# Sixteen-head attention with a ternary-weight layer: input tiles loaded from another queue, in four buffers instead of three

## The chip, the cores and the metric

One Trainium2 chip, eight cores. Each core runs the same program on one of the eight batch elements, and nothing is exchanged between cores. The metric is the device time of the slowest core, in microseconds (us), as the median over runs. Engines are called PE (TensorE, matmul), PEld (its weight loads), DVE (VectorE), ACT (ScalarE), POOL (GpSimd) and SP (SyncE). SP does no arithmetic here: it issues transfers. Each engine takes its instructions strictly in the order of its own program, and an instruction that waits holds up all behind it.

## The reference

Per batch element, with S = E = 2048, 16 heads of 128:

```python
xn = layernorm(x)                                    # over E, no scale or shift
q, k, v = xn @ wq, xn @ wk, xn @ wv                  # 16 heads of 128
q, k = rope(q), rope(k)
attn = softmax(q @ k.T / sqrt(128) + causal) @ v @ wo
s = mean(abs(weight)); w_t = clip(round(weight / s), -1, 1)
ffn = xn @ (w_t * s).T + bias
out = x + attn + ffn
```

## The kernel before

Five lists of closures are built, one for each engine, and then played back, so the order of the Python calls is the order of each engine's program. There are two phases. Phase 1 makes the transposed layernorm `xnT`, does projections and attention for the 16 heads, and in the shadow of the heads makes the ternary weights. Phase 2 (L961 and L977) multiplies out both output products and isn't touched.

**Layernorm.** `plan_ln_tile(tt)` (L218) handles 128 rows of x: a 1 MB load into `xst[tt % 3]`, four statistics instructions and an aggregate on DVE (L233 to L242), Ln and Exp on ACT (L251, L258), the subtract and multiply to bf16 `xnn[tt % 2]` on DVE (L267), and a DMA transpose from `xnn` into `xnT`, issued by SP. The load is issued by POOL. It waits only for its buffer (`xst_free`: the L267 of the tile that last used it) and for the buffer's own semaphore.

**Heads 0 and 1** are interleaved with the layernorm (L726 to L760). p0(c) and p1(c) are the projections of chunk c (512 columns) for heads 0 and 1: K, Q and V in that order, 16 matmuls each, alternating between the banks `pA` and `pB`. p0(c) has to wait for the four transposes of its chunk. After p1(c) comes b0(c), the layernorm of the four tiles of chunk c+1, and then the attention of chunk c. SP also issues a DMA transpose of V (`vh<-prawv`, here called tv) for each head and chunk, as soon as DVE has evacuated V (L515).

**Heads 2 to 15** (L777) have the order: p(0), p(1), attention(0), background(0), background(1), p(2), attention(1), background(2), p(3), attention(2), attention(3), background(3). The background of heads 2 to 5 is `plan_quantA_tile` (L292): load 1 MB of the layer's weight, take its absolute sum on ACT (L306), one tile for each chunk. The background of heads 6 to 13 is `plan_quantB_tile` (L368), two tiles a head: load 1 MB again, three DVE instructions (L391, L395, L401), then on SP a DMA transpose (`wtTs<-wtbf`) and, once that has landed, a store. Sixteen tiles go through each of the two.

**Who waits behind these.** In DVE's program the three instructions of a quantB tile stand between the masks of attention(c-1) (L617) and the evacuation of K of the next chunk (L515). The V projection of that chunk writes the same bank as its K projection, so PE waits until K is evacuated. In ACT's program a quantA tile stands between two attentions' exponentials (L606). In SP's program tv of chunk c stands ahead of all that background(c) issues.

**Head weights.** `plan_head_weights` (L420) has POOL load the wq, wk and wv slices of a head, with a cast from f32 to bf16, in the same POOL program as the tile loads. Each waits for the load before it on its semaphore.

Of the kernel before, what the change touches and what calls it, by code (L numbers as in the profile page):

```python
# [8 lines left out]
F32 = mybir.dt.float32  # L9
# [30 lines left out]
def build_nc():  # L40
# [26 lines left out]
    with ctx:  # L67
# [21 lines left out]
        biasbc = sb("biasbc", [128, E], BF16)  # L89
        ctx1 = ExitStack()  # L90
        sb1 = lambda n_, s_, d_: ctx1.enter_context(nc.sbuf_tensor(n_, s_, d_))
        xst = [sb1(f"xst{i}", [128, E], F32) for i in range(3)]
        xnn = [sb1(f"xnn{i}", [128, E], BF16) for i in range(2)]
        wtbf = [sb1("wtbf0", [128, E], BF16)] * 4
        wtTs = [sb1("wtTs0", [128, NT * 128], BF16)] * 4
# [40 lines left out]
        def dma(engname, sem_name, make_out_in, extra_waits=(), ordered=True):  # L136
            prev = cnt[sem_name] if ordered else 0
            ws = tuple(extra_waits)

            @on(engname)  # L140
            def _(e, sem_name=sem_name, prev=prev, ws=ws, make_out_in=make_out_in):
                for s_, v_ in ws:
                    if v_:
                        e.wait_ge(sems[s_], v_)  # L144
                if prev:
                    e.wait_ge(sems[sem_name], prev)  # L146
                out, in_, tp = make_out_in()
                if tp:
                    e.dma_start_transpose(out, in_).then_inc(sems[sem_name], 16)
                else:  # L150
                    e.dma_start(out=out, in_=in_).then_inc(sems[sem_name], 16)  # L151
            return bump(sem_name, 16)

        for dst, src in [(c2, c2_d), (s2, s2_d), (tri, tri_d), (onc, onc_d),
                         (oncf, oncf_d), (onrf, onrf_d), (onm, onm_d)]:
            dma("sync", "c", (lambda dst=dst, src=src: (dst[:, :], src, False)),
                ordered=False)
        consts_c = cnt["c"]
        dma("gpsimd", "bias", (lambda: (biasb[:, :], bias_d, False)),
            ordered=False)  # L160
        dma("gpsimd", "bias", (lambda: (onr[:, :], onr_d, False)),
            ordered=False)
        bias_v = cnt["bias"]

        @on("vector")
        def _(e):
# [43 lines left out]
        def _(e):  # L210
            e.wait_ge(sems["c"], consts_c)

        xst_free = [("dv", 0), ("dv", 0), ("dv", 0)]
        xnn_free = [("txn", 0), ("txb", 0)]
        ln_state = {"prev_aggr": 0}
        ln_prev = [0, 0, 0]

        def plan_ln_tile(tt):  # L218
            b = tt % 3
            b2 = tt % 2  # L220
            xs = "x%d" % b
            my_x = dma("gpsimd", xs,
                       (lambda tt=tt, b=b: (xst[b][:, :],
                        bass.AP(x_d.tensor, tt * 128 * E, [[E, 128], [1, E]]), False)),
                       extra_waits=[xst_free[b]])

            @on("vector")
            def _(e, b=b, xs=xs, my_x=my_x, prev_aggr=ln_state["prev_aggr"]):
                e.wait_ge(sems[xs], my_x)
                if prev_aggr:  # L230
                    e.wait_ge(sems["dv"], prev_aggr)
                for j in range(3):
                    e.bn_stats(st6[:, 6 * j:6 * j + 6], xst[b][:, 512 * j:512 * (j + 1)])  # L233
                e.bn_stats(st6[:, 18:24], xst[b][:, 1536:2048]).then_inc(sems["dv"], 1)
            dv_stats = bump("dv")

            @on("vector")
            def _(e, b=b, dv_stats=dv_stats, prev=ln_prev[b]):
                e.wait_ge(sems["dv"], dv_stats)
                if prev:  # L240
                    e.wait_ge(sems["dv"], prev)
                e.bn_aggr(mv[b][:, :], st6[:, :]).then_inc(sems["dv"], 1)  # L242
            dv_aggr = bump("dv")
            ln_state["prev_aggr"] = dv_aggr

            @on("scalar")
            def _(e, b=b, dv_aggr=dv_aggr, prev=ln_prev[b]):
                e.wait_ge(sems["dv"], dv_aggr)
                if prev:
                    e.wait_ge(sems["dv"], prev)  # L250
                e.activation(out=rstd[b][:, :], in_=mv[b][:, 1:2], func=AF.Ln,  # L251
                             bias=epsv[:, :]).then_inc(sems["ac"], 1)
            ac_ln = bump("ac")

            @on("scalar")
            def _(e, b=b, ac_ln=ac_ln):
                e.wait_ge(sems["ac"], ac_ln)
                e.activation(out=rstd[b][:, :], in_=rstd[b][:, :], func=AF.Exp,  # L258
                             scale=-0.5).then_inc(sems["ac"], 1)
            ac_rstd = bump("ac")  # L260

            @on("vector")
            def _(e, b=b, b2=b2, ac_rstd=ac_rstd, xf=xnn_free[b2]):
                e.wait_ge(sems["ac"], ac_rstd)
                if xf:
                    e.wait_ge(sems[xf[0]], xf[1])
                e.tensor_scalar(out=xnn[b2][:, :], in0=xst[b][:, :], scalar1=mv[b][:, 0:1],  # L267
                                scalar2=rstd[b][:, :], op0=ALU.subtract,
                                op1=ALU.mult).then_inc(sems["dv"], 1)
            dv_xn = bump("dv")  # L270
            xst_free[b] = ("dv", dv_xn)
            ln_prev[b] = dv_xn

            txs = "txn" if tt % 2 == 0 else "txb"
            xnn_free[b2] = (txs, dma("sync", txs,
                              (lambda tt=tt, b2=b2: (
                                  bass.AP(xnT, tt * 128, [[NT * S, 128], [S, NT], [1, 128]]),
                                  xnn[b2][:, :], True)),
                              extra_waits=[("dv", dv_xn)]))

        plan_ln_tile(0)
        plan_bias_copies()
        for tt in range(1, 4):
            plan_ln_tile(tt)
        xnT_ready = 16 * (NT // 2)

        qa_ac = [0] * NT
# [2 lines left out]
        quantB_state = {"prev_sub": 0}  # L290

        def plan_quantA_tile(qt):  # L292
            b = qt % 3
            b2 = qt % 2
            xs = "x%d" % b
            my_x = dma("gpsimd", xs,
                       (lambda qt=qt, b=b: (xst[b][:, :],
                        bass.AP(wf_d.tensor, qt * 128 * E, [[E, 128], [1, E]]), False)),
                       extra_waits=[xst_free[b]])

            @on("scalar")
            def _(e, qt=qt, b=b, b2=b2, xs=xs, my_x=my_x):
                e.wait_ge(sems[xs], my_x)
                e.wait_ge(sems["txn"], xnT_ready)
                e.wait_ge(sems["txb"], xnT_ready)
                e.activation(out=xnn[b2][:, :], in_=xst[b][:, :], func=AF.Abs,  # L306
                             accum_out=accw[:, qt:qt + 1]).then_inc(sems["ac"], 1)
            qa_ac[qt] = bump("ac")
            xst_free[b] = ("ac", qa_ac[qt])
# [56 lines left out]
            return bump("dv")  # L366

        def plan_quantB_tile(qt, thr_dv):  # L368
            b = qt % 3
            xs = "x%d" % b  # L370
            my_x = dma("gpsimd", xs,
                       (lambda qt=qt, b=b: (xst[b][:, :],
                        bass.AP(wf_d.tensor, qt * 128 * E, [[E, 128], [1, E]]), False)),
                       extra_waits=[xst_free[b]])

            wtbf_free = (("tw%d" % ((qt - 1) % 2)), qb_tw[qt - 1]) if qt >= 1 else None
            prev_sub = quantB_state["prev_sub"]
# [42 lines left out]
        def plan_head_weights(h, gate_pe):  # L420
            out = {}
            hb = h % 2
            for wd, dsts, s_ in ((wq_d, wslq, "wq"), (wk_d, wslk, "wk"), (wv_d, wslv, "wv")):
                if DBG_NO_WSL:
                    out[s_] = cnt[s_]
                    continue
                out[s_] = dma("gpsimd", s_,
                              (lambda wd=wd, dst=dsts[hb], h=h: (dst[:, :],
                               bass.AP(wd.tensor, h * 128, [[E, 128], [E * 128, NT], [1, 128]]),
                               False)),  # L430
                              extra_waits=[("pe", gate_pe)])
            return out
# [38 lines left out]
        def make_head(h):  # L471
# [224 lines left out]

            def plan_background(c, h=h):
                if h == 0 and c < CH - 1:
                    for t2 in range(4 * (c + 1), 4 * (c + 1) + 4):
                        plan_ln_tile(t2)  # L700
                if do_quant and n_heads >= 14:
                    if 2 <= h <= 5:
                        plan_quantA_tile(4 * (h - 2) + c)
                    elif h == 6 and c == 0:
                        quant_thr_dv[0] = plan_quant_reduce()
                        rs_gate_pe_extra[0] = nonlocal_holder.get("rs_pe", 0)
                        plan_quantB_tile(0, quant_thr_dv[0])
                    elif 6 <= h <= 13 and c % 2 == 0 and not (h == 6 and c == 0):
                        plan_quantB_tile(2 * (h - 6) + c // 2, 0)
# [390 lines left out]
```

## Time and profile before

| | us |
|---|---|
| median of 2 runs | 1821.25 (1814.53 to 1827.96) |
| the profiled execution, device time | 1812.49 |
| its slowest core (core 0), first to last instruction | 1810.9 |
| its fastest core (core 2) | 1793.1 |
| PE busy in that core 0 | 1527.9 (84%) |
| DVE busy | 760.1 (42%) |
| ACT busy | 478.3 (26%) |

Times in the rows are microseconds from the start of the core's span. A row of the timeline has the start, the time taken, the engine, the line, the operation, what is written `<-` what is read, and how many instructions are merged; brackets give the idle time before it and what ended it. SPq and the like are the instructions that issue transfers, and their time is that of issuing, not of the transfer. All plain transfers are issued from L151 and all DMA transposes from L149.

### The profile page before, as it was taken

The page shows a single profiled execution, that of the slowest core. Times are in us where ns is not written, and L with a number is a line of the kernel's source. Part 1 is how long each engine was busy: PE and PEld are TensorE (multiplying, and loading weights), DVE is VectorE, ACT ScalarE, POOL GpSimd, SP SyncE. Part 2 cuts the span into 40 slices and gives each one's busy share as a digit, 9 for nine tenths or more (in the row PEclk, how much of TensorE's full clock was granted, in tenths as well). Part 3 has the DMA queues.
Part 4 walks back from the last instruction along what each step waited for, and adds up shares of the span by engine and source line. Part 5 has one row for each costly group of instructions (what it writes and reads, how often), then busy time and mean ns, then how long its engine had stood idle before and what let it go on. Part 6 is the DMA issues. An engine that isn't in the chain of part 4 may idle for free. (4 is left out here: it accounts for less than half of the span.)

```text
span 1810.9 us, 29591 instructions; the slowest of 8 cores (1793.1 to 1810.9 us)
## 1 busy us (share of the span) xinstructions
PE 1527.9 (84%) x9096; PEld 880.1 (49%) x9096; DVE 760.1 (42%) x1559; ACT 478.3 (26%) x837; POOL 101.2 (6%) x118
## 2 busy tenths in 40 slices
PE   0515459999999899989999999999919999999999
PEld 0202224444444344434444444444408888888888
DVE  3516253544535447456465474454302222222222
ACT  1001125345454351443433524514500000000000
POOL 2000001101100100010010000000000000000000
PEclk9857679999999999999999999999969999999999
DMA  9994536547366783673644734600084687786772
GB/s 203 165 104 63 86 73 111 78 101 114 72 116 70 122 134 78 89 108 95 101 88 92 121 79 56 88 21 7 10 179 110 147 190 161 171 170 133 156 158 86
DMA packets 350420, 194.93 MB, mean 108 GB/s; under 512 B 240193, under 2 KB 338498, under 8 KB 343874
## 3 DMA queue, kind: packets, MB, share of 16 engines
q0 software_dynamic: 139072, 92.29, 32.6%
q1 hardware_dynamic: 157730, 63.53, 19.5%
q10 hardware_dynamic: 53472, 37.23, 7.1%
q8 instruction: 84, 1.38, 0.3%
q14 instruction: 62, 0.51, 0.1%
HBM read 177.28 MB, written 32.51 MB: 116 GB/s over the span
## 5 line engine op out<-in xcount | busy, mean ns | idle before, releaser
L606 ACT ACTIVATE et<-pC,bias 128x512 bf16<-128x512 f32 (+3 forms) x240 | 149.9, 625 | 591.3 <-PE pC L593 590.4
L643 PE MATMUL pF<-et,onms 128*128 128x512 bf16 (+3 forms) x640 | 226.3, 355 | 38.1 <-DVE et L617 23.3
L593 PE MATMUL pC<-qTh,kTh 128*128 128x512 bf16 (+3 forms) x240 | 84.3, 351 | 112.0 <-ACT et L606 112.0
L500 PE MATMUL pA<-xnT,wslk 128*128 128x512 bf16 x480 | 119.3, 405 | 66.0 <-DMA xnT<-xnn 65.7
L617 DVE TENSOR_TENSOR et<-et,trim 128x128 bf16<-128x128 bf16 x256 | 56.7, 225 | 273.6 <-ACT et L606 270.4
L961 PE MATMUL pA<-wtc,xnT 128*128 128x256 bf16 x1024 | 123.9, 275 | 13.3 <-DMA wtc<-wtT_scr 13.1
L645 PE MATMUL pG<-et,vh 128*128 128x512 bf16 x376 | 133.9, 360 | 0.0
L977 PE MATMUL pA<-woc,oTh 128*128 128x256 bf16 x896 | 109.7, 275 | 27.3 <-DMA oTh<-outT_scr 27.3
L606 ACT ACTIVATE et<-pD,bias 128x512 bf16<-128x512 f32 (+3 forms) x208 | 130.7, 628 | 3.8 <-PE pD L593 3.3
L643 PEld LDWEIGHTS pF<-et,onms 128*128 128x128 bf16 x640 | 63.2, 99 | 137.6 <-issue 91.7
L961 PE MATMUL pB<-wtc,xnT 128*128 128x256 bf16 x1024 | 122.6, 273 | 0.0
L1000 DVE TENSOR_TENSOR osl<-pA,xsl 128x256 f32<-128x256 f32 x64 | 27.2, 424 | 224.3 <-PE pA L977 129.0
L606 ACT ACTIVATE et<-pH,bias 128x512 bf16<-128x512 f32 (+1 forms) x192 | 118.5, 617 | 4.6 <-PE pH L593 3.9
L961 PEld LDWEIGHTS pA<-wtc,xnT 128*128 128x128 bf16 x1024 | 100.7, 99 | 26.1 <-issue 13.7
L500 PE MATMUL pB<-xnT,wslk 128*128 128x512 bf16 x480 | 108.8, 379 | 0.2
L500 PE MATMUL pA<-xnT,wslv 128*128 128x512 bf16 x480 | 108.8, 379 | 0.0
L500 PE MATMUL pA<-xnT,wslq 128*128 128x512 bf16 x480 | 108.8, 379 | 0.0
L500 PE MATMUL pB<-xnT,wslq 128*128 128x512 bf16 x480 | 108.8, 379 | 0.0
L500 PE MATMUL pB<-xnT,wslv 128*128 128x512 bf16 x480 | 108.8, 379 | 0.0
L500 PEld LDWEIGHTS pA<-xnT,wslk 128*128 128x128 bf16 x480 | 47.7, 103 | 125.6 <-issue 81.0
L977 PE MATMUL pB<-woc,oTh 128*128 128x256 bf16 x896 | 108.3, 272 | 0.0
L977 PEld LDWEIGHTS pA<-woc,oTh 128*128 128x128 bf16 x896 | 88.3, 99 | 38.4 <-issue 27.8
(99 smaller groups left out, 1869.2 us busy)
## 6 DMA issues: line engine op xcount, KB each, us to landing
xst<-wf POOLq DMA_DIRECT2D x32, 1024.0 KB, 10.8
xst<-x POOLq DMA_DIRECT2D x16, 1024.0 KB, 18.0
xsl<-x SPq DMA_DIRECT2D x128, 128.0 KB, 4.1
wtc<-wtT_scr ACTq DMA_DIRECT2D x16, 1024.0 KB, 11.4
woc<-wo POOLq DMA_DIRECT2D x16, 1024.0 KB, 13.4
y<-osl ACTq DMA_DIRECT2D x128, 128.0 KB, 3.6
wslq<-wq POOLq DMA_DIRECT2D x16, 512.0 KB, 10.8
wslk<-wk POOLq DMA_DIRECT2D x16, 512.0 KB, 13.8
```

Source lines behind the costliest of these rows:

```text
L500: e.matmul(pp[:, 0:CW], wsl[:, it * 128:(it + 1) * 128], bass.AP(xnT, it * S + c * CW, [[NT * S, 128], [1, CW]]), start=(it == 0), stop=False)
L593: e.matmul(pc_[:, col0:CW], kTh[hb][:, kt * 128:(kt + 1) * 128], bass.AP(qTh[hb], cs0 + col0, [[S, 128], [1, n]]), start=True, stop=True). ...
L606: e.activation(out=et[slot][:, col0:CW], in_=pc_[:, col0:CW], func=AF.Exp, scale=INV_SQRT_D, bias=bias3[:, :]).then_inc(sems["ac"], 1)
L617: e.tensor_tensor(out=et[slot][:, col0:col0 + 128], in0=et[slot][:, col0:col0 + 128], in1=tri[:, :], op=ALU.mult).then_inc(sems["dv"], 1)
L643: e.matmul(pF[:, col0:CW], onm[:, :], et[slot][:, col0:CW], start=(kt == 0), stop=(kt == nkt - 1))
L645: e.matmul(pv[:, col0:CW], vh[hb][:, kt * 128:(kt + 1) * 128], et[slot][:, col0:CW], start=(kt == 0), stop=(kt == nkt - 1)).then_inc(sems[ ...
L961: e.matmul(pp[:, 0:W2], bass.AP(xnT, it * S + tt * 128, [[NT * S, 128], [1, 128]]), wtc[ecb][:, it * W2:(it + 1) * W2], start=(it == 0), s ...
L977: mm = e.matmul(pp[:, 0:W2], lh, woc[ecb][:, it * W2:(it + 1) * W2], start=False, stop=(it == NT - 1))
L1000: e.tensor_tensor(out=osl[ob][:, :], in0=pp[:, 0:W2], in1=xsl[tb][:, :], op=ALU.add).then_inc(sems["dv"], 1)
```

## The change

- `xst` has four buffers in place of three (tile number modulo 4). `mv` and `rstd` stay at three.
- All loads into `xst`, of x and of the layer's weight, go through a new `plan_x_load` and are issued by SP in place of POOL. They have the same kind of waits as before: the buffer's last reader, and the buffer's semaphore.
- The loads of x tiles 0 to 3 stand first in SP's program, ahead of the constants (two of 1 MB each and five small ones). In b0(c) the four loads stand together, ahead of the four tiles' transposes.
- In quantA and quantB the load stands in SP's program where the tile is planned: behind tv of the chunks projected so far, ahead of the tile's own transpose and store.
- POOL now issues only the bias, the head weights and, in phase 2, wo. The head weights go in the order k, q, v in place of q, k, v.

```diff
-        xst = [sb1(f"xst{i}", [128, E], F32) for i in range(3)]
+        xst = [sb1(f"xst{i}", [128, E], F32) for i in range(4)]
...
+        xst_free = [("dv", 0), ("dv", 0), ("dv", 0), ("dv", 0)]
+
+        def plan_x_load(tt, src_d=x_d):
+            b = tt % 4
+            return dma("sync", "x%d" % b,
+                       (lambda tt=tt, b=b, src_d=src_d: (xst[b][:, :],
+                        bass.AP(src_d.tensor, tt * 128 * E, [[E, 128], [1, E]]), False)),
+                       extra_waits=[xst_free[b]])
+
+        xl03 = [plan_x_load(tt) for tt in range(4)]
         for dst, src in [(c2, c2_d), (s2, s2_d), (tri, tri_d), (onc, onc_d),
...
-        def plan_ln_tile(tt):
-            b = tt % 3
+        def plan_ln_tile(tt, my_x=None):
+            b = tt % 4
+            b3 = tt % 3
             b2 = tt % 2
             xs = "x%d" % b
-            my_x = dma("gpsimd", xs,
-                       (lambda tt=tt, b=b: (xst[b][:, :],
-                        bass.AP(x_d.tensor, tt * 128 * E, [[E, 128], [1, E]]), False)),
-                       extra_waits=[xst_free[b]])
+            if my_x is None:
+                my_x = plan_x_load(tt)
...
         def plan_quantA_tile(qt):
-            b = qt % 3
+            b = qt % 4
...
-            my_x = dma("gpsimd", xs,
...
+            my_x = plan_x_load(qt, src_d=wf_d)
...
         def plan_quantB_tile(qt, thr_dv):
-            b = qt % 3
+            b = qt % 4
             xs = "x%d" % b
-            my_x = dma("gpsimd", xs,
...
+            my_x = plan_x_load(qt, src_d=wf_d)
...
-            for wd, dsts, s_ in ((wq_d, wslq, "wq"), (wk_d, wslk, "wk"), (wv_d, wslv, "wv")):
+            for wd, dsts, s_ in ((wk_d, wslk, "wk"), (wq_d, wslq, "wq"), (wv_d, wslv, "wv")):
...
                 if h == 0 and c < CH - 1:
-                    for t2 in range(4 * (c + 1), 4 * (c + 1) + 4):
-                        plan_ln_tile(t2)
+                    t2s = list(range(4 * (c + 1), 4 * (c + 1) + 4))
+                    mxs = [plan_x_load(t2) for t2 in t2s]
+                    for t2, mx in zip(t2s, mxs):
+                        plan_ln_tile(t2, mx)
```

## Rows read from the trace of the kernel before

**Rows 1.** The page, busy tenths of PE and its granted clock in 40 slices.

```profile
PE   0515459999999899989999999999919999999999
PEclk9857679999999999999999999999969999999999
```

**Rows 2.** Windows: length, busy of PE, PEld, DVE, ACT, POOL, clock, DMA share, GB/s.

```profile
78.00:132.00 54.00, 2.56 (x9) 1.15 (x9) 16.70 (x29) 4.89 (x14) 2.12 (x4) 0.52 1.04 119
159.00:208.00 49.00, 7.09 (x25) 2.75 (x24) 17.25 (x30) 7.65 (x18) 2.11 (x4) 0.56 0.93 131
```

**Rows 3.** Timeline of the start, up to the first projection.

```profile
1.07 0.39 SPq L151 DMA_DIRECT2D c<-c2t  x1
14.23 1.88 DVE L233 BATCH_NORM_STATS2 st<-xst 128x6 f32<-128x512 f32 x3 [13.00 <-DMA xst<-x]
20.65 26.18 SPq L149 DMA_TRANSPOSE xnT<-xnn  x4
53.55 6.32 PE L500 MATMUL pA<-xnT,wslk 128*128 128x512 bf16 x15 [31.23 <-DMA xnT<-xnn]
```

**Rows 4.** Timeline of b0(0), the layernorm of tiles 4 to 7.

```profile
50.65 1.63 POOL L151 DMA_DIRECT2D xst<-x  x3
78.13 1.87 DVE L233 BATCH_NORM_STATS2 st<-xst 128x6 f32<-128x512 f32 x3
83.90 0.53 POOL L151 DMA_DIRECT2D xst<-x  x1 [31.62 <-DVE xnn L267]
107.70 1.35 DVE L267 TENSOR_SCALAR xnn<-xst,mv,rstd 128x2048 bf16<-128x2048 f32 x1 [11.46 <-DMA xnT<-xnn]
132.24 6.22 PE L500 MATMUL pA<-xnT,wslk 128*128 128x512 bf16 x15 [20.51 <-DMA xnT<-xnn]
```

**Rows 5.** Timeline of b0(2), the layernorm of tiles 12 to 15.

```profile
237.81 1.87 DVE L233 BATCH_NORM_STATS2 st<-xst 128x6 f32<-128x512 f32 x3
257.42 1.35 DVE L267 TENSOR_SCALAR xnn<-xst,mv,rstd 128x2048 bf16<-128x2048 f32 x1 [0.91 <-ACT rstd L258]
266.16 3.40 PE L500 MATMUL pA<-xnT,wslk 128*128 128x512 bf16 x15 [0.23 <-issue]
```

**Rows 6.** Timeline of DVE, SP and PE around one head's two quantB tiles.

```profile
770.00 0.69 DVE L515 CAST prawv<-pB 128x512 bf16<-128x512 f32 x1
770.82 1.19 SPq L149 DMA_TRANSPOSE vh<-prawv  x1
772.25 1.34 DVE L391 TENSOR_SCALAR xnn<-xst,thrv,sclv 128x2048 bf16<-128x2048 f32 x1
775.23 1.23 DVE L401 TENSOR_TENSOR wtbf<-xnn 128x2048 bf16<-128x2048 bf16 x1 [0.17 <-DVE xnn L395]
776.65 0.69 DVE L515 CAST prawk<-pA 128x512 bf16<-128x512 f32 x1 [0.20 <-PE pA L503]
779.76 3.40 PE L500 MATMUL pA<-xnT,wslv 128*128 128x512 bf16 x15
783.56 0.69 DVE L515 CAST prawv<-pA 128x512 bf16<-128x512 f32 x1
784.38 2.63 SPq L149 DMA_TRANSPOSE vh<-prawv  x1
795.69 3.40 PE L500 MATMUL pB<-xnT,wslv 128*128 128x512 bf16 x15
```

**Rows 7.** Transfers in heads 6 to 13: count, size, median us from issue to landing.

```profile
xst<-wf POOLq DMA_DIRECT2D x13, 1024.0 KB, 6.3
```

**Rows 8.** Timeline of PE in attention(3) of that head, after two gaps.

```profile
810.53 0.59 PE L643 MATMUL pF<-et,onms 128*128 128x512 bf16 x1 [0.56 <-DMA vh<-prawv]
813.87 0.38 PE L593 MATMUL pC<-qTh,kTh 128*128 128x512 bf16 x1
```

**Rows 9.** Timeline of ACT around two quantA tiles.

```profile
346.48 1.89 ACT L306 ACTIVATE xnn<-xst 128x2048 bf16<-128x2048 f32 x1
353.89 0.69 ACT L606 ACTIVATE et<-pC,bias 128x512 bf16<-128x512 f32 x1 [5.42 <-PE pC L593]
```

More of the change, by code:

```diff
@@ L152, in dma @@
             return bump(sem_name, 16)
+        dma("gpsimd", "bias", (lambda: (biasb[:, :], bias_d, False)),
+            ordered=False)
+        dma("gpsimd", "bias", (lambda: (onr[:, :], onr_d, False)),
+            ordered=False)
+        bias_v = cnt["bias"]
+        xst_free = [("dv", 0), ("dv", 0), ("dv", 0), ("dv", 0)]
[6 more added lines that the diff above has]
+        xl03 = [plan_x_load(tt) for tt in range(4)]
         for dst, src in [(c2, c2_d), (s2, s2_d), (tri, tri_d), (onc, onc_d),
@@ L158, in build_nc @@
         consts_c = cnt["c"]
[L159 to L163, printed above, removed]
         @on("vector")
@@ L211, in _ @@
             e.wait_ge(sems["c"], consts_c)
-        xst_free = [("dv", 0), ("dv", 0), ("dv", 0)]
         xnn_free = [("txn", 0), ("txb", 0)]
@@ L237, in _ @@
             @on("vector")
-            def _(e, b=b, dv_stats=dv_stats, prev=ln_prev[b]):
+            def _(e, b3=b3, dv_stats=dv_stats, prev=ln_prev[b3]):
                 e.wait_ge(sems["dv"], dv_stats)
@@ L241, in _ @@
                     e.wait_ge(sems["dv"], prev)
-                e.bn_aggr(mv[b][:, :], st6[:, :]).then_inc(sems["dv"], 1)
+                e.bn_aggr(mv[b3][:, :], st6[:, :]).then_inc(sems["dv"], 1)
             dv_aggr = bump("dv")
@@ L246, in _ @@
             @on("scalar")
-            def _(e, b=b, dv_aggr=dv_aggr, prev=ln_prev[b]):
+            def _(e, b3=b3, dv_aggr=dv_aggr, prev=ln_prev[b3]):
                 e.wait_ge(sems["dv"], dv_aggr)
@@ L250, in _ @@
                     e.wait_ge(sems["dv"], prev)
-                e.activation(out=rstd[b][:, :], in_=mv[b][:, 1:2], func=AF.Ln,
+                e.activation(out=rstd[b3][:, :], in_=mv[b3][:, 1:2], func=AF.Ln,
                              bias=epsv[:, :]).then_inc(sems["ac"], 1)
@@ L255, in _ @@
             @on("scalar")
-            def _(e, b=b, ac_ln=ac_ln):
+            def _(e, b3=b3, ac_ln=ac_ln):
                 e.wait_ge(sems["ac"], ac_ln)
-                e.activation(out=rstd[b][:, :], in_=rstd[b][:, :], func=AF.Exp,
+                e.activation(out=rstd[b3][:, :], in_=rstd[b3][:, :], func=AF.Exp,
                              scale=-0.5).then_inc(sems["ac"], 1)
@@ L262, in _ @@
             @on("vector")
-            def _(e, b=b, b2=b2, ac_rstd=ac_rstd, xf=xnn_free[b2]):
+            def _(e, b=b, b3=b3, b2=b2, ac_rstd=ac_rstd, xf=xnn_free[b2]):
                 e.wait_ge(sems["ac"], ac_rstd)
@@ L266, in _ @@
                     e.wait_ge(sems[xf[0]], xf[1])
-                e.tensor_scalar(out=xnn[b2][:, :], in0=xst[b][:, :], scalar1=mv[b][:, 0:1],
-                                scalar2=rstd[b][:, :], op0=ALU.subtract,
+                e.tensor_scalar(out=xnn[b2][:, :], in0=xst[b][:, :], scalar1=mv[b3][:, 0:1],
+                                scalar2=rstd[b3][:, :], op0=ALU.subtract,
                                 op1=ALU.mult).then_inc(sems["dv"], 1)
@@ L271, in plan_ln_tile @@
             xst_free[b] = ("dv", dv_xn)
-            ln_prev[b] = dv_xn
+            ln_prev[b3] = dv_xn
             txs = "txn" if tt % 2 == 0 else "txb"
@@ L279, in plan_ln_tile @@
                               extra_waits=[("dv", dv_xn)]))
-        plan_ln_tile(0)
+        plan_ln_tile(0, xl03[0])
         plan_bias_copies()
         for tt in range(1, 4):
-            plan_ln_tile(tt)
+            plan_ln_tile(tt, xl03[tt])
         xnT_ready = 16 * (NT // 2)
@@ L292, in plan_quantA_tile @@
         def plan_quantA_tile(qt):
-            b = qt % 3
+            b = qt % 4
             b2 = qt % 2
             xs = "x%d" % b
-            my_x = dma("gpsimd", xs,
-                       (lambda qt=qt, b=b: (xst[b][:, :],
-                        bass.AP(wf_d.tensor, qt * 128 * E, [[E, 128], [1, E]]), False)),
-                       extra_waits=[xst_free[b]])
+            my_x = plan_x_load(qt, src_d=wf_d)
             @on("scalar")
@@ L368, in plan_quantB_tile @@
         def plan_quantB_tile(qt, thr_dv):
-            b = qt % 3
+            b = qt % 4
             xs = "x%d" % b
-            my_x = dma("gpsimd", xs,
-                       (lambda qt=qt, b=b: (xst[b][:, :],
-                        bass.AP(wf_d.tensor, qt * 128 * E, [[E, 128], [1, E]]), False)),
-                       extra_waits=[xst_free[b]])
+            my_x = plan_x_load(qt, src_d=wf_d)
             wtbf_free = (("tw%d" % ((qt - 1) % 2)), qb_tw[qt - 1]) if qt >= 1 else None
```

## The prediction, made before the run

> **What bounds the kernel now.** I read the page first. The slices of PE [rows 1] show two parts. From slice 7 on (45.3 us each) PE is busy over 80% in nearly every slice, so there the kernel runs at PE's pace, and only what makes PE wait counts. In the first six slices PE is half idle. The windows of that part [rows 2] show where: in 78 to 132 us PE works 2.6 of 54 us, and in 159 to 208 us 7.1 of 49, while no engine is busy even 20 us. So I went to the timeline. The first projection starts at 53.55 us, and what ended its wait is a transpose into `xnT` [rows 3]. The second chunk's does the same at 132.24 [rows 4]. The layernorm of tiles 4 to 7 starts on DVE at 78.13, but the last tile's L267 waits 11.5 us for an earlier transpose to free `xnn`, and PE gets its chunk 54.1 us after the layernorm began. For tiles 12 to 15 the same work takes far less: DVE starts at 237.81, its last L267 at 257.42 waits for no transfer, and PE goes on at 266.16, after 28.4 us [rows 5]. The difference is beside it, on POOL. While tiles 4 to 7 are being transposed, POOL loads the next x tiles, as each L267 frees a buffer (the first at 83.90) [rows 4]. While tiles 12 to 15 are transposed only one x tile is left to load.
>
> Second part, heads 6 to 13. The view to read is DVE, SP and PE together [rows 6]. DVE starts the quantB tile at 772.25 with no wait, since POOL had loaded it long before. It ends at 776.46, and K is evacuated by 777.34. PE wants the bank for V at 779.76. The slack is thus 2.4 us.
>
> **The change, part by part.**
>
> Start. x tile 0 now leaves at about 1.1 us, ahead of the constants, and doesn't queue behind them. Its landing taken as 6.3 us [rows 7] puts the first statistics at 7.4 instead of 14.23 [rows 3]. But the same megabytes and the head weights, now issued from about 3 us, still have to share the DMA engines with the four transposes before 53.55, and the transposes queue behind x1 to x3 and 2 MB of constants. Of the 6.9 us I take 4. Bounds: 12 us (the whole early start, and head weights out of the way of the transposes) and a loss of 4 (transposes held by the constants).
>
> b0(0), b0(1), b0(2). The loads of these four tiles now stand in SP's program behind tv of p1(c), and that waits for V's evacuation, the very instruction after which DVE wants the tile. tv begins 0.1 us after V is evacuated and takes 1.19 us to issue [rows 6]; then the load, 6.3 us. So each layernorm starts 1.3 + 0.1 + 6.3 = 7.7 us late. In return no x load of a later chunk runs beside the transposes, and I price the rest as in [rows 5], 28.4 us. Each then takes 36.1 us. Against 54.1 for b0(0) that is 18.0 gained. For b0(1) the window [rows 2] gives 49 less 0.8 before DVE starts, 48.2: 12.1 gained. b0(2) already takes 28.4: 7.7 lost. Sum with the start: 4 + 18 + 12 - 8 = 26 us gained. Bounds: if the transposes are slow for another reason, the three lose 7.7 each and the sum is a loss of 19; if the landing is 4.4 us and the start gives all, the gain is 12 + 20 + 14 - 6 = 40. The 4.4 comes from [rows 3]: three megabytes (two of constants, x tile 0) are in by 14.23 after an issue at 1.07.
>
> Here a rule fits. The Trainium skill (DMA: Bandwidth & Descriptors, Queues, rings and completion order) says that each DMA engine takes turns between its queues, and that a semaphore increment lands only after all earlier writes of that engine, from whatever queue. By that, a transpose beside a load on POOL's queue is counted as landed late, and [rows 4] against [rows 5] agree. By the same page the descriptors of one queue start in order, so the transpose of tile 4 would stand behind the load of tile 7: three more megabytes after tile 4's landing, where the layernorm of tile 4 covers about half of it. That would take some 6 us off each of the two gains.
>
> quantB, 16 tiles in 8 heads. This is where the change costs. POOL fetched the tile so early that DVE never waits at 772.25. SP can't: its program is held at tv(1) until V is evacuated at 770.69, and tv(1) is issued by 772.01. The load leaves at 772.1 and lands at 778.4 [rows 6, 7]. The three DVE instructions take 4.2 us (772.25 to 776.46), so K is evacuated at 782.6 + 0.8 = 783.4. PE wanted the bank at 779.76: a stall of 3.6 us. Second tile: from the start of K's evacuation to the end of V's is 7.6 us (776.65 to 784.25), so V is out at 790.3. tv(2) takes 1.2 to 2.6 us to issue, the load leaves at about 792.4, lands at 798.7, and K is evacuated at 798.7 + 4.2 + 0.8 = 803.7. PE wants the bank at 795.69 + 3.6 = 799.3: 4.4 us. Both: 8.0 us a head. Nothing can hide it, as PE's program is in order and DVE's too. Two more costs. PE's clock: after gaps of some 2 us, the eight matmuls from 810.53 to 813.87 took 3.34 us where eight at full rate (0.215 apart) take 1.72 [rows 8], so 1.6 us lost, at the lower of the two clock levels (1.2 GHz of 2.4). Each new gap is longer, so either may cost that; I take one of two, 1.6. And tv(3) leaves later against attention(3), which already waited 0.56 us for it [rows 8]; it now stands behind a later transpose of the tile: 0.5, at most 3. Sum 8.0 + 1.6 + 0.5 = 10.1 a head, 81 us for eight. Bounds: landing 4.4 gives 1.7 + 2.3 = 4.0 a head and no clock cost, 32 us; landing 7, both clock drops and 3 for tv give about 16, 125 us.
>
> A load issued by SP may be quicker than one by POOL. The Trainium skill (DMA: Bandwidth & Descriptors, SWDGE vs HWDGE) gives the first byte as about 0.6 us against 1: by that the 16 waits would be 0.4 shorter, 6 us in all; no row here has the two side by side.
>
> quantA, 16 tiles in 4 heads. Here ACT waits. In the head shown, the second absolute sum ends at 348.5 and the exponentials resume at 353.89 [rows 9], 5.4 us of slack. The head is built as in [rows 6], where the load leaves 2.4 us after p(1) ends and PE comes back to attention(1) some 13.6 us after. Two loads behind one another land at about 8.7 and 12.4 after p(1) (3.7 apart, three megabytes in 11 us at the start), and the sum takes 2.1: 14.5 against about 13.8. That is 0.7 late, for four heads 3 us; bounds 0 and 10. The loads of background(2) and (3) have the longer attentions as cover.
>
> Fourth buffer, order k, q, v, and POOL's freed program: nothing. PE's first need, wk, now loads before the transposes that it waits for anyway; a fourth buffer lets loads leave earlier only where they waited for a buffer, and on SP they wait for tv instead.
>
> **Sum.** -26 + 81 + 3 = +58 us, against the profiled execution's 1812.5: 1870, or 3.2% more. That execution is 0.5% under the median of the runs shown.
>
> **The rivals.**
> - *The small stall.* SP's load lands in about 4.4 us and the clock holds. quantB costs 32, the rest stays: 1812.5 + 32 + 3 - 26 = 1822. For it: the start's three megabytes. Against: 6.3 is the median of 13 of just these loads.
> - *No gain at the start.* The transposes were slow by themselves, or are as slow behind loads on their own queue. 1812.5 + 81 + 3 + 19 = 1916. For it: in 159 to 208 us the DMA share is 0.93 at 131 GB/s only [rows 2], as if transposes alone could do it. Against: [rows 5].
> - *The other side: the load is there in time.* If a load issued at 772.1 landed within 2.5 us, K would be evacuated by 779.8 and no bank would be late. Then only the start counts: 1812.5 - 26 = 1787, at best 1772. It decides at 2.5 us of landing; at 6.3 it is far.
>
> **How the numbers follow.** The forecast 0.58, small stall 0.22, no gain 0.14, in time 0.06. A measurement tells about 2%, 36 us, from no change. Nine tenths of the forecast's weight lie above +36 us (0.52), the rest is within; no gain is all slower (0.14); the small stall (+9) is within 2%; in time is within 2% for a third of it. Faster 0.04, same 0.30, slower 0.66. The range reaches from half-way between the small stall and its best start (26 to 40 us gained), 1815, to the no-gain case, 1916, and leaves the tails. The likeliest one's own range is 1848 to 1895.
>
> **What would show each step.** In the trace after: first statistics near 7 us; chunk 1 reaching PE some 36 us after its layernorm begins to wait, likewise chunk 2; in heads 6 to 13 DVE idle before L391 for about 6 us, ended by the load, 16 times, and PE idle before the V projection 3 to 5 us, 16 times; the last statistics of b0(2) late by 7 to 8 us. If DVE doesn't wait at L391, or the wait is under 2.5 us, the forecast falls. If the windows of b0(0) and b0(1) still last 50 us, the gain at the start was misread.

## The result and the profile after

The changed kernel takes 1842.58 us (median of 11 runs) against 1818.32 for the kernel before (10 runs): ratio 1.0128, 95% interval 1.0097 to 1.0159, so about 23 us slower. The forecast was 1870, 3.2% slower. The direction held; in per cent, the size was two and a half times too large. Some executions of any of these kernels run longer with one die at a lower clock; the ratios leave them out.

The page of the changed kernel, its slowest core, busy tenths of PE and the granted clock (compare [rows 1]):

```profile
span 1833.1 us, 29589 instructions; the slowest of 8 cores (1814.7 to 1833.1 us)
...
PE   0543489999999888888889988899938999999999
...
PEclk9967889999999999999999999999968999999999
```

Each slice is 45.8 us. Slice 3 went from 1 to 4 and slice 6 from 5 to 8, and eleven of the slices 14 to 26 show 8 where before only 14 and 18 did: a gain at the start, a loss in heads 6 to 13. To put numbers to it I took the start of each stage's first matmul from the trace (the two kernels issue the same matmuls in the same order), as means over the six cores whose matmul records are complete in both. The last row ends with the last matmul, and "forecast, change" is what the prediction adds for that stage:

| stage | before, us | after, us | forecast, change | measured, change |
|---|---|---|---|---|
| start to p0(0) | 57.5 | 58.1 | -4 | +0.6 |
| b0(0): end of p1(0) to p0(1) | 52.5 | 33.8 | -18 | -18.7 |
| b0(1) | 47.0 | 34.4 | -12 | -12.6 |
| b0(2) | 29.8 | 36.7 | +8 | +6.9 |
| start to p2(0), all of the above with the projections | 318.8 | 291.6 | -26 | -27.2 |
| heads 2 to 5 (quantA) | 280.2 | 279.7 | +3 | -0.5 |
| head 6 | 76.4 | 76.4 | +10 | 0.0 |
| heads 7 to 13, each | 70.8 | 77.7 | +10.1 | +6.9 |
| heads 14, 15 and phase 2 | 630.6 | 629.7 | 0 | -0.9 |
| whole | 1801.5 | 1821.4 | +58 | +19.9 |

So the start came out near the forecast in sum, and the miss is in quantB: 7 x 6.9 = 48 us, not 81. Single cores scatter: b0(0) takes 45.1 to 59.7 us on the six cores before and 32.6 to 34.6 after.

The windows of b0(0), b0(1) and b0(2) after, to set beside [rows 2]:

```profile
84.10:117.80 33.70, 2.56 (x9) 1.12 (x9) 16.59 (x28) 4.89 (x14) 0.00 (x0) 0.56 0.73 191
145.70:179.30 33.60, 5.65 (x21) 2.20 (x21) 16.95 (x28) 6.46 (x16) 0.00 (x0) 0.59 0.70 191
207.40:243.60 36.20, 8.00 (x33) 3.27 (x33) 16.95 (x28) 8.96 (x20) 0.00 (x0) 0.62 0.63 178
```

PE and DVE do what they did before, in 34 us in place of 54 and 49, and 191 GB/s move where 119 and 131 did. The timeline of b0(0) after, DVE, SP and PE, answers to [rows 4]:

```profile
85.49 3.34 SPq L151 DMA_DIRECT2D xst<-x  x4
...
92.75 1.88 DVE L242 BATCH_NORM_STATS2 st<-xst 128x6 f32<-128x512 f32 x3 [8.67 <-DMA xst<-x]
...
111.80 1.35 DVE L276 TENSOR_SCALAR xnn<-xst,mv,rstd 128x2048 bf16<-128x2048 f32 x1 [0.91 <-ACT rstd L267]
...
117.84 5.66 PE L503 MATMUL pA<-xnT,wslk 128*128 128x512 bf16 x15 [2.02 <-DMA xnT<-xnn]
```

DVE now waits 8.7 us for the load, the new wait, and none of the four L276 (the old L267) waits for a transpose, the old one.

One head with its quantB tiles after, SP, DVE and PE, beside [rows 6]:

```profile
758.77 1.35 DVE L394 TENSOR_SCALAR xnn<-xst,thrv,sclv 128x2048 bf16<-128x2048 f32 x1 [5.46 <-DMA xst<-wf]
...
762.88 0.68 DVE L518 CAST prawk<-pA 128x512 bf16<-128x512 f32 x1
...
763.71 5.08 PE L503 MATMUL pA<-xnT,wslv 128*128 128x512 bf16 x15 [2.78 <-DVE prawk L518]
...
769.46 0.68 DVE L518 CAST prawv<-pA 128x512 bf16<-128x512 f32 x1
...
770.28 1.18 SPq L149 DMA_TRANSPOSE vh<-prawv  x1
...
771.61 0.46 SPq L151 DMA_DIRECT2D xst<-wf  x1
...
777.01 1.35 DVE L394 TENSOR_SCALAR xnn<-xst,thrv,sclv 128x2048 bf16<-128x2048 f32 x1 [2.97 <-DMA xst<-wf]
...
781.13 0.68 DVE L518 CAST prawk<-pB 128x512 bf16<-128x512 f32 x1
...
781.96 3.40 PE L503 MATMUL pB<-xnT,wslv 128*128 128x512 bf16 x15 [0.47 <-DVE prawk L518]
...
787.71 0.68 DVE L518 CAST prawv<-pB 128x512 bf16<-128x512 f32 x1
...
788.52 1.21 SPq L149 DMA_TRANSPOSE vh<-prawv  x1
...
798.04 0.38 PE L646 MATMUL pF<-et,onms 128*128 128x512 bf16 x1 [1.65 <-DMA vh<-prawv]
```

Read it from the top. DVE waits 5.5 us for the first tile; PE waits 2.8 for DVE's evacuation of K; and then 15 matmuls of V take 5.08 us where they take 3.40 at the full clock. The second tile keeps DVE waiting 3.0 us, but PE only 0.47. Then V leaves DVE at 788.4, tv(3) leaves at 788.5, and attention(3) waits 1.65 us for it. The waits of that core between 628 and 1190 us (total, times, longest) say the same for all heads:

```profile
DVE xnn L394 <- DMA xst<-wf: 60.1, 14, 6.2
...
PE pA L503 <- DVE prawk L518: 19.9, 7, 3.5
...
PE pF L646 <- DMA vh<-prawv: 6.8, 4, 1.9
...
PE pB L503 <- DVE prawk L518: 3.9, 7, 0.8
```

And the transfers in the same stretch (count, size, median to landing) beside [rows 7]:

```profile
xst<-wf SPq DMA_DIRECT2D x14, 1024.0 KB, 5.3
...
vh<-prawv SPq DMA_TRANSPOSE x29, 2.4
```

### The profile page after: what moved, and what is told of

Same layout as the page of the kernel before. It is cut to its first block and busy times, and to the rows that moved or that the text cites. A ratio compares the mean times of both kernels' runs of the same rounds, so it can differ in the third digit from the quotient of the medians.

```text
span 1833.1 us, 29589 instructions; the slowest of 8 cores (1814.7 to 1833.1 us)
## 1 busy us (share of the span) xinstructions
PE 1539.4 (84%) x9096; PEld 881.1 (48%) x9096; DVE 756.2 (41%) x1559; ACT 480.1 (26%) x837; POOL 74.6 (4%) x70
## 5 line engine op out<-in xcount | busy, mean ns | idle before, releaser
L646 PE MATMUL pF<-et,onms 128*128 128x512 bf16 (+3 forms) x640 | 227.6, 357 | 26.9 <-ACT et L609 11.5
L503 PE MATMUL pA<-xnT,wslk 128*128 128x512 bf16 x480 | 113.1, 389 | 34.8 <-DMA xnT<-xnn 34.4
L503 PE MATMUL pA<-xnT,wslv 128*128 128x512 bf16 x480 | 120.4, 408 | 19.9 <-DVE prawk L518 19.9
L966 PE MATMUL pA<-wtc,xnT 128*128 128x256 bf16 x1024 | 123.9, 275 | 12.3 <-DMA wtc<-wtT_scr 11.5
L982 PE MATMUL pA<-woc,oTh 128*128 128x256 bf16 x896 | 109.7, 275 | 24.4 <-DMA oTh<-outT_scr 24.4
L1005 DVE TENSOR_TENSOR osl<-pA,xsl 128x256 f32<-128x256 f32 x64 | 27.2, 425 | 215.8 <-PE pA L982 126.6
L596 PEld LDWEIGHTS pC<-qTh,kTh 128*128 128x128 bf16 x240 | 23.7, 99 | 185.5 <-issue 167.3
L966 PEld LDWEIGHTS pB<-wtc,xnT 128*128 128x128 bf16 x1024 | 100.5, 98 | 12.0
## 6 DMA issues: line engine op xcount, KB each, us to landing
wtc<-wtT_scr ACTq DMA_DIRECT2D x16, 1024.0 KB, 11.2
wslk<-wk POOLq DMA_DIRECT2D x16, 512.0 KB, 11.4
```

The costliest lines, as they stand in the source:

```text
L503: e.matmul(pp[:, 0:CW], wsl[:, it * 128:(it + 1) * 128], bass.AP(xnT, it * S + c * CW, [[NT * S, 128], [1, CW]]), start=(it == 0), stop=False)
L596: e.matmul(pc_[:, col0:CW], kTh[hb][:, kt * 128:(kt + 1) * 128], bass.AP(qTh[hb], cs0 + col0, [[S, 128], [1, n]]), start=True, stop=True). ...
L646: e.matmul(pF[:, col0:CW], onm[:, :], et[slot][:, col0:CW], start=(kt == 0), stop=(kt == nkt - 1))
L966: e.matmul(pp[:, 0:W2], bass.AP(xnT, it * S + tt * 128, [[NT * S, 128], [1, 128]]), wtc[ecb][:, it * W2:(it + 1) * W2], start=(it == 0), s ...
L982: mm = e.matmul(pp[:, 0:W2], lh, woc[ecb][:, it * W2:(it + 1) * W2], start=False, stop=(it == NT - 1))
L1005: e.tensor_tensor(out=osl[ob][:, :], in0=pp[:, 0:W2], in1=xsl[tb][:, :], op=ALU.add).then_inc(sems["dv"], 1)
```

## The experiments

Two questions: is quantB's loss the place of the load in SP's program, or the queue; and what made the transposes slow before. Ratios are against the kernel before, with their 95% intervals; stage lengths are means as in the table above. The expectations give p(2), p(3) and attention(3) between bounds that lie two matmuls early, and so 0.1 to 0.4 us shorter than the lengths here (10.0 for 10.4, 14.6 for 14.9). The differences agree to 0.1 us.

**quant_on_pool.** The change, with quantA's and quantB's loads given back to POOL, on semaphores of their own (g0 to g3):

```diff
-            xs = "x%d" % b
-            my_x = plan_x_load(qt, src_d=wf_d)
+            xs = "g%d" % b
+            my_x = plan_x_load(qt, src_d=wf_d, q="gpsimd")
```

> The changed kernel, with only the loads of quantA and quantB given back to POOL (semaphores of their own); x tiles stay on SP. Theory A (the whole loss is that SP reaches quantB's loads too late): the 48 us that heads 6 to 13 cost more come back and the 27 us of the start stay, so about 27 us below the kernel before, ratio 0.985; DVE no longer waits at the first quantB instruction, a head is 70.8 us again. Rival B (the loss comes from POOL's and SP's transfers sharing DMA engines in another way, or from the head weights' new order): most of the loss stays, ratio 1.00 to 1.012.

Measured 1789.75 us, ratio 0.9877 (0.9836 to 0.9917). A head of 7 to 13 takes 70.9 us. The view of waits has no line for the load; DVE starts both tiles of a head with none:

```profile
756.96 1.35 DVE L394 TENSOR_SCALAR xnn<-xst,thrv,sclv 128x2048 bf16<-128x2048 f32 x1
...
773.06 1.35 DVE L394 TENSOR_SCALAR xnn<-xst,thrv,sclv 128x2048 bf16<-128x2048 f32 x1
```

Theory A holds; this kernel already beats both. It gains 22 us and not the 27 that were expected: p2(0) starts at 297.1 us, where the change has 291.6. Four of these 5.5 us are a longer wait before head 2's first projection, and the runs do not show why.

**before_quantB_on_sp.** The other way round: the kernel before, with quantB's loads alone on SP.

```diff
-            my_x = dma("gpsimd", xs,
+            my_x = dma("sync", xs,
```

> The kernel before, with only the quantB loads issued by SP, at the place in its program that the change gives them; three buffers, x and quantA loads stay on POOL. Theory A: all of the loss and none of the gain, +48 us, ratio 1.026, and in each head p(2) near 14.6 us against 10.0, p(3) near 11.0 against 10.2, attention(3) 1.5 us longer. Rival B (the loss needs the other parts of the change as well): ratio under 1.015.

Measured 1872.47 us, ratio 1.034 (1.0265 to 1.0415). A head takes 78.3 us, with p(2) 15.3, p(3) 11.4 and attention(3) 13.9, close to the change (14.9, 11.2, 13.9). The loss needs no other part of the change. The ratio is above the 1.026 expected: in the profiled execution heads 7 to 13 cost 52 us, and p2(0) starts 5 us later than in the kernel before, though the edit touches nothing ahead of it. That part is scatter or unexplained.

**quantB_on_sp_ahead.** The change, with quantB's loads still on SP's queue, but two tiles ahead in SP's program.

```diff
-            my_x = plan_x_load(qt, src_d=wf_d)
+            my_x = q_ahead.pop(qt)
...
                             extra_waits=[(tw, qb_tw[qt])])
+            if qt + 2 < NT:
+                q_ahead[qt + 2] = plan_x_load(qt + 2, src_d=wf_d)
```

> The changed kernel with quantB's loads still on SP's queue, but each placed in SP's program two tiles ahead (right behind the store of the tile two before). Theory A (place, not queue): as good as on POOL, ratio 0.985. Rival C (on SP's queue the megabyte holds up the transposes of V and of the tile, wherever it stands): a loss of the size of attention(3)'s 1.5 us and more a head stays, ratio 0.99 to 1.01.

Measured 1791.69 us, ratio 0.9878 (0.9841 to 0.9915), a head 71.3 us, with p(2) and p(3) at 10.4 as before the change. Place, not queue: of rival C at most 0.4 us a head is left, in attention(3) (12.9 against 12.5). This kernel keeps quantA on SP, late, and its heads 2 to 5 take 280.0 us against 280.5 with quantA on POOL: that part costs nothing.

**first_tile_on_sp and second_tile_on_sp.** `quant_on_pool` with only one of a head's two quantB tiles loaded by SP at the change's place, to split the 6.9 us.

```diff
-            xs = "g%d" % b
-            my_x = plan_x_load(qt, src_d=wf_d, q="gpsimd")
+            xs = ("x%d" if qt % 2 == 0 else "g%d") % b
+            my_x = plan_x_load(qt, src_d=wf_d, q="sync" if qt % 2 == 0 else "gpsimd")
```

> quant_on_pool with only the first quantB tile of each head (the one ahead of p(2)) loaded by SP at its place in the change. If the measured 6.9 us a head are p(2)'s stall and what follows from it, p(2) is 14.6 us against 10.0, p(3) stays at 10.2, and attention(3) shows whether its 1.5 us come from this tile; a head 75.4 us or more against 70.9.

> quant_on_pool with only the second quantB tile of each head (the one ahead of p(3)) loaded by SP. Reading I (the forecast's 4.4 us of stall was wrong because the tile's own distance, V's evacuation to the bank's need, is longer than its load): V evacuated, 1.2 us of tv, 5.3 of landing and 4.8 on DVE end within 0.5 us of PE's need, so p(3) is 10.2 to 10.8 us and no clock is lost. Reading II (the forecast's terms, with no first stall ahead: landing 6.3, tv up to 2.6): p(3) near 13 us. Attention(3) is 1.5 us longer if that cost comes with this tile.

| heads 7 to 13, mean, us | p(2) | p(3) | attention(3) | head |
|---|---|---|---|---|
| both on POOL | 10.4 | 10.4 | 12.5 | 70.9 |
| first on SP | 14.7 | 10.4 | 11.9 | 74.6 |
| second on SP | 10.4 | 11.4 | 14.8 | 74.2 |
| both (the change) | 14.9 | 11.2 | 13.9 | 77.7 |

Ratios 1.0026 (0.9978 to 1.0074) and 1.0031 (1.0008 to 1.0054). The first tile costs 3.7 us a head: 4.3 in p(2), less 0.6 in attention(3). The second costs 3.3, of which 1.0 is its own bank wait and 2.3 is attention(3), which waits for the transpose of V. Reading I is right about p(3) on four of the six cores, where a p(3) takes 10.4 to 11.7 us. On cores 3 and 7 it takes 11.4 to 15.4. On core 7 the same load lands after 7.2 us in the median (first block, the transfers), not 5.3, and DVE and PE wait for it (second block, the timeline):

```profile
xst<-wf SPq DMA_DIRECT2D x7, 1024.0 KB, 7.2
```

```profile
782.67 1.35 DVE L394 TENSOR_SCALAR xnn<-xst,thrv,sclv 128x2048 bf16<-128x2048 f32 x1 [4.78 <-DMA xst<-wf]
...
787.61 3.40 PE L503 MATMUL pB<-xnT,wslv 128*128 128x512 bf16 x15 [2.28 <-DVE prawk L518]
...
804.74 0.58 PE L646 MATMUL pF<-et,onms 128*128 128x512 bf16 x1 [2.85 <-DMA vh<-prawv]
```

So the second tile sits at the edge: with the load in 5.3 us it nearly hides, and each further microsecond of landing is a microsecond of stall (over the 42 second tiles of heads 7 to 13, without the three that also lost the clock, p(3) grows by 0.97 us for each us of landing). Why those two cores are slower isn't shown.

**before_buf4_kqv.** The kernel before with four buffers, the order k, q, v and the grouped planning, but all loads on POOL and the constants first.

```diff
-            return dma("sync", "x%d" % b,
+            return dma("gpsimd", "x%d" % b,
```

> The kernel before with four buffers, k, q, v order and the loads of each b0 grouped ahead of its tiles, but all on POOL and constants first. Prediction's step: these parts are worth nothing, ratio 0.995 to 1.005. Rival: a fourth buffer lets one more x load run beside the transposes and b0(0) and b0(1) get longer, ratio up to 1.01, or it takes the last load away from b0's end and they get shorter, down to 0.99.

Measured 1819.69 us, ratio 1.0035 (1.0006 to 1.0064). b0(0) takes 51.8 us and b0(1) 48.4, against 52.5 and 47.0 before. These parts gain nothing; the interval allows a loss of up to 0.6%.

**x_on_pool_late.** `quant_on_pool`, with the x loads of b0 on POOL too, but held until V of p1(c) is evacuated.

```diff
-                    mxs = [plan_x_load(t2) for t2 in t2s]
+                    mxs = [plan_x_load(t2, q="gpsimd", late=[("dv", cnt["dv"])]) for t2 in t2s]
```

> quant_on_pool with the x loads of b0(0), b0(1), b0(2) also issued by POOL, but only once V of p1(c) is evacuated, so at the same time as SP issues them in the changed kernel. Theory D (the start gains because no x load runs beside the transposes; the queue does not matter): b0 still takes 33 to 37 us from the first wait of DVE, the same time as quant_on_pool within 5 us. Rival E (the gain comes from the loads being on SP's own queue, in order with the transposes): b0(0) and b0(1) take near 50 us, 20 to 30 us slower than quant_on_pool.

Measured 1793.2 us, ratio 0.9844 (0.9786 to 0.9903). b0 takes 33.7, 34.2 and 37.1 us, the change's lengths to 0.4 us. So POOL's queue is as good as SP's if no load runs beside the transposes. Theory D so far.

**x_on_sp_interleaved.** `quant_on_pool`, with x tile t+4 loaded by SP right behind the transpose of tile t: loads beside transposes again, on one queue.

```diff
-                    mxs = [plan_x_load(t2) for t2 in t2s]
-                    for t2, mx in zip(t2s, mxs):
-                        plan_ln_tile(t2, mx)
+                    for t2 in range(4 * (c + 1), 4 * (c + 1) + 4):
+                        plan_ln_tile(t2, ahead.pop(t2))
+                        if t2 + 4 < NT:
+                            ahead[t2 + 4] = plan_x_load(t2 + 4)
```

> quant_on_pool with x tile t+4 loaded by SP right behind the transpose of tile t, so that loads run beside transposes as they did before the change, but on the one queue. Theory D (a load beside transposes slows them, on whatever queue): b0(0) and b0(1) go back to 45 to 54 us, ratio 0.99 to 1.00. Rival F (only a load on the other queue slows them): no wait for the load and four transposes each held by one megabyte, b0 28 to 33 us, 10 to 20 us faster than quant_on_pool.

Measured 1778.67 us, ratio 0.9776 (0.9704 to 0.9847). b0 takes 29.3, 29.8 and 29.6 us, so D in its general form falls and F stands. The eight transposes into `xnT` that have a load beside them, issue to landing (min, median, max): first in the kernel before (60 to 235 us), then in `before_buf4_kqv` (60 to 235), which has four buffers as this kernel has, then in this kernel (60 to 190):

```profile
DMA to landing us min/median/max: 8.4/19.5/30.2
```

```profile
DMA to landing us min/median/max: 12.1/19.0/28.8
```

```profile
DMA to landing us min/median/max: 4.4/6.7/7.7
```

The loads themselves, in the kernel before (80 to 200 us) and in this one (88 to 170):

```profile
DMA to landing us min/median/max: 8.1/19.0/24.0
```

```profile
DMA to landing us min/median/max: 5.3/5.8/6.3
```

And the window of b0(0) in this kernel, beside the first of [rows 2]:

```profile
83.50:113.00 29.50, 3.73 (x16) 1.55 (x14) 17.52 (x30) 4.89 (x14) 0.00 (x0) 0.59 0.79 192
```

The same megabytes run beside the same transposes. A load leaves 0.5 us after its transpose's issue begins in the first two kernels, and some 2 to 5 us after in this one. From POOL's queue the loads stretch a transpose's median landing to 19 us and take as long themselves. From SP's queue a transpose lands in 6.7 us (4.4 with no load beside it), a load in 5.8. With POOL's loads the DMA engines are busy all the time (share 1.04) at 119 GB/s; here they are busy for 0.79 of 29.5 us, at 192.

**x_on_sp_ahead.** `quant_on_pool`, with the next four x loads as a batch behind the last transpose, while PE projects.

```diff
+                    for t2 in range(4 * (c + 2), min(4 * (c + 2) + 4, NT)):
+                        ahead[t2] = plan_x_load(t2)
```

> quant_on_pool with the four x loads of the next b0 issued by SP as a batch right behind the last transpose of this one, while PE does p0(c) and p1(c). No overlap with transposes of xnT, and no wait of DVE at the tile. Both D and F: b0 takes 28.4 us as b0(2) did before, 3 times 5 to 8 us less than quant_on_pool, ratio 0.975. If the transposes of V behind 4 MB of loads hurt, attention(0) starts late and the gain is under 10 us.

Ratio 0.9722 (0.9651 to 0.9792), about 50 us under the kernel before; the profiled execution took 1768.81 us. b0 takes 25.9, 26.9 and 29.3 us: the 8.7 us wait of DVE is gone, and the first two are 1.5 to 2.5 us under the 28.4 of [rows 5]. The transposes of V behind 4 MB of loads do no harm here.

**bias_copies_last.** `quant_on_pool`, with `plan_bias_copies()` moved behind the first four tiles. The reason is a chain at the start of the changed kernel, here PE, ACT and DVE:

```profile
27.36 0.58 PE L207 MATMUL pH<-biasb,onrs 1*128 1x512 bf16 x1 [15.67 <-DMA onms<-onm]
...
28.03 0.60 ACT L214 ACTIVATE biasbc<-pH 128x512 bf16<-128x512 f32 x1 [13.87 <-PE pH L207]
...
29.28 1.34 DVE L276 TENSOR_SCALAR xnn<-xst,mv,rstd 128x2048 bf16<-128x2048 f32 x1 [12.31 <-ACT rstd L267]
```

The constants, now behind 4 MB of x, arrive at 27.3 us. PE's last bias matmul waits for them, ACT's copy waits for PE, and the second tile's Ln stands behind that copy in ACT's program.

> quant_on_pool with the ACT copies of the bias moved behind the first four layernorm tiles. In the changed kernel ACT's second tile waits 12.3 us at the start, behind a copy that waits for PE, which waits for the constants, now last in SP's queue. Theory G (that chain holds the first projection): p0(0) starts near 50 us instead of 57 to 60, 8 us faster. Rival H (the start is bound by the megabytes that share the DMA engines): p0(0) moves by less than 2 us, no difference in time.

Measured 1785.92 us, ratio 0.9826 (0.9774 to 0.9877); against `quant_on_pool` alone the intervals overlap. p0(0) starts at 54.2 us instead of 59.1, as a mean. DVE in this kernel, second and third tile:

```profile
17.69 1.35 DVE L276 TENSOR_SCALAR xnn<-xst,mv,rstd 128x2048 bf16<-128x2048 f32 x1 [0.86 <-ACT rstd L267]
...
33.77 1.34 DVE L276 TENSOR_SCALAR xnn<-xst,mv,rstd 128x2048 bf16<-128x2048 f32 x1 [11.99 <-DMA xnT<-xnn]
```

The second tile comes 11.6 us sooner, and then the third waits 12.0 us for the first transpose. G holds for 5 us of its 8; the rest goes to H: the transposes are now what the start waits for.

**ahead_and_bias_last.** The last two together.

> x_on_sp_ahead and bias_copies_last together, quant loads on POOL. If the two gains are independent (14 to 20 us from the loads ahead, 5 from the start): 20 to 25 us under quant_on_pool, near 1765 us, ratio 0.970. If the start is bound by bytes, the four loads that follow the first transposes eat the 5 us.

Ratio 0.9756 (0.9718 to 0.9794); the profiled execution took 1766.37 us. p0(0) is at 56.4 us, against 58.5 with the batch alone. No gain over `x_on_sp_ahead` is shown. Either is 2.4 to 2.8% under the kernel before.

## Why the prediction was right or wrong

**The start, right in its sum, in part by luck.** Forecast -26, measured -27.2 us. The cause was right. The changes of the three layernorms were each priced to within 1 us: -22 in sum, measured -24.4. Inside them two misses offset each other: DVE waited 8.7 us for the load and not 7.7, and the rest of b0(0) took 25 us and not the 28.4 of [rows 5] (25.9 in `x_on_sp_ahead`, which has no wait). The first 4 us weren't there (+0.6). Against that stand 3.4 us that the sum did not have, mainly a p0(2) shorter by 1.8 us and a wait before head 2 shorter by 1.5.

The reason stated with [rows 4] and [rows 5], x loads from POOL beside transposes, was tested in both directions: taking the overlap away on POOL's own queue gives 34 us, and moving it to SP's queue gives 29. So it takes both, the overlap and the other queue. The load was priced at 6.3 us after a 1.4 us start; with four issued together the first took about 7.3. For the first 4 us I named the constants behind x only as a load on the queue, and did not follow who waits for them: PE, through it ACT, and through it the second tile, 12.3 us. That is a place where a stall should have been followed to the next waiter.

The rule of the Trainium skill (DMA: Bandwidth & Descriptors, Queues, rings and completion order), that an increment lands only after all earlier writes of that engine from any queue, agrees in sign: the transposes that wait beside POOL's loads are the ones reported late. The runs do not show that it accounts for the size. The 6 us that the prediction would take off for loads ahead of the transposes on one queue did not show: the first transpose of b0(0) is issued at 98.05 us, 4 us before the last of the four loads lands, and takes 5.8 us where the other three take 4.3.

**quantB, right in kind, too large by 33 us.** The stall, its cause and its place were as forecast: the load is held behind tv, DVE waits at the first quantB instruction 14 times for 4.3 us in the mean, PE before the V projection. By terms, a head:

| term, us a head | forecast | measured |
|---|---|---|
| p(2): stall and clock | 3.6 + 1.6 | 4.6 (2.8 and 1.7 in the head shown) |
| p(3): stall | 4.4 | 0.9 |
| attention(3), waiting for V | 0.5 | 1.5 |
| sum | 10.1 | 6.9 |

The step that failed is "PE wants the bank at 795.69 + 3.6 = 799.3: 4.4 us". From the start of p(2)'s V projection to the need of the next bank there are 17.6 us in the trace after (763.71 to 781.3), not 15.9 (783.4 to 799.3): the V projection ran at the lower clock and took 1.7 us more. I booked the clock's cost as a loss and forgot that it delays the next need as well. On the other side, from the same point to the end of K's evacuation, I had 20.3 us and the trace has 18.1 (763.71 to 781.81): the load landed in 5.3 us, not 6.3, and left 7.9 us after the start of V, not 9.0, as V was evacuated 0.5 us sooner and tv(2) took 1.2 us to issue, not the mean of 1.2 and 2.6. So 20.3 - 15.9 = 4.4 became 18.1 - 17.6 = 0.5. This is a difference of two long intervals, and an error of 10% in either is the whole result. The 6.3 of [rows 7] is a median over two kinds of load: on six cores of the kernel before, the 36 issued with nothing of POOL's just ahead landed in 6.1 us, the 30 issued behind a head's three weights in 15.6. `second_tile_on_sp` shows the supply side by itself: with no first stall ahead, p(3) loses 1.0 us on average, with the landing as the lever. That the clock's loss puts off the need is read from the trace of the change; no run isolates it.

Attention(3) was too small. I took tv(3) as held by the tile's own transpose. It is held by DVE: after the second tile DVE works off K, Q and V late. It begins on V 2.3 us after PE has finished it (785.4 to 787.71), where in [rows 6] it begins 0.35 us after (783.21 to 783.56). So tv(3) is issued 4.9 us before attention(3) begins and not 6.8 (medians of 42 heads). It runs beside the head weights' loads, as it did before the change, and lands in 8.6 us against 7.7 (9.5 in the head shown, 788.5 to 798.0). It comes with the second tile alone.

Head 6 was counted at 10 us and cost 2 at most: it takes 76.4 us in the change, 74.7 in `quant_on_pool`, and 76.4 in the kernel before, where one core of 82.5 lifts the mean (the other five average 75.2). With the first tile alone on SP it takes 74.9, with the second alone 77.5, so in this head, where the weights' scale and threshold are worked out ahead of the first tile, that tile costs nothing.

**quantA, right:** +3 with bounds 0 and 10; measured -0.5. ACT waited for these loads 12 times, 19.0 us in all, but inside its slack.

**The fourth buffer and the order k, q, v, right:** no gain in `before_buf4_kqv`.

**The rivals.** "The small stall", +9 us, named a landing of 4.4 us and a clock that holds. The landing was 5.3 and the clock did not hold, but the change of +23 lies nearer to it than to the +58 forecast. (Its 2.3 us for the second stall should read 2.5 by its own terms, 4.4 less 1.9, so its quantB is 34 us and not 32.) "No gain at the start" fell, and "the load is there in time" fell. The Trainium skill (DMA: Bandwidth & Descriptors, Latency and other measured facts) has SP's path 0.4 us faster to the first byte. Here the same megabyte landed 0.8 us faster from SP, 5.3 against the 6.1 of POOL's loads with nothing just ahead of them, which agrees in sign.

## What to carry to other kernels

An engine program that holds waits for one stream is a bad place for another stream's prefetch: a load goes where nothing ahead of it waits for the present, or it goes ahead in the program, as `quantB_on_sp_ahead` did at 0.4 us a head. Before moving a load to another queue, ask what else that queue will be held by and, apart from that, what will run beside it: here the same move gained 27 us by one and lost 48 us by the other. When a second stall follows a first, draw both intervals anew from the point where the first ended, the clock's loss included, since it delays the need as well as the supply.

## What the runs showed of the hardware

- DMA transposes with a 1 MB load beside each: landing in 19.5 us (median) with the loads on POOL's queue and three buffers, 19.0 with four, 6.7 with the loads on SP's own queue, and 4.4 with no load beside. The loads took 19.0 us from POOL and 5.8 from SP. The runs do not show the mechanism.
- That holds while POOL issues nothing else. At the start of the changed kernel, with the constants ahead on SP's queue and POOL's head weights beside, the first transpose took 19.7 us.
- A 1 MB load issued by POOL landed in 6.1 us with nothing of its own queue just ahead, and in 15.6 behind a head's three weights.
- After a gap of 2.4 to 3.9 us before p(2)'s V projection, 7 to 9 of its 16 matmuls ran at half pace in 39 of 42 heads, 1.3 to 1.7 us lost; in two heads none did, in one 14. Fifteen matmuls took 5.08 us in place of 3.40.
- The same 1 MB load from SP in the same kernel landed in 5.3 us on one core and 7.2 on another.
